# A four-layer gated cross-attention kernel: where the second layer's blocks stand in their slots, and how the last output tiles wait

## What is computed

```
queries = rope(q @ Wq.T)            # 32 heads of 128
keys    = rope(ctx @ Wk.T)          # 8 key heads, each serves 4 query heads
values  = ctx @ Wv.T
scores  = queries @ keys.T * 128 ** -0.5, causal mask (256 x 256)
x = x + tanh(g) * (softmax(scores) @ values) @ Wd.T
```

## Time and profile before

| what | us |
|---|---|
| median of 3 runs (lowest, highest) | 2197.25 (2195.84, 2198.91) |
| the profiled execution, its own time | 2194.48 |
| its span in the profile | 2192.7 |
| TensorE matmul busy | 1983.3 |
| VectorE busy | 1470.3 |
| ScalarE busy | 1026.8 |
| GpSimd busy | 927.6 |

### The profile page before, as it was taken

One profiled execution on the slowest core, in us unless ns is written; L12 is line 12 of the kernel. 1 busy time (PEld: TensorE's weight loads), 2 busy tenths in 40 slices (PEclk: granted clock), 3 DMA queues, 4 the chain that ended last, 5 costly groups with the idle time before them and its releaser, 6 DMA issues.

```text
span 2192.7 us, 33276 instructions
## 1 busy us (share of the span) xinstructions
PE 1983.3 (90%) x10874; PEld 1660.7 (76%) x10874; DVE 1470.3 (67%) x2725; ACT 1026.8 (47%) x2264; POOL 927.6 (42%) x971
## 2 busy tenths in 40 slices
PE   5999999999747999997997999997889999999998
PEld 4788888887536777776665888886678888888886
DVE  5777777777767777776423555555557766777676
ACT  3666666666414444444112544443145545555542
POOL 2555455544535555455231323322234444444432
PEclk9999999999968999999997999999799999999999
DMA  3212222121310211111110101001101110111001
GB/s 137 64 54 73 87 72 72 47 84 54 97 34 30 78 48 52 48 48 54 48 55 25 33 9 32 17 10 55 53 10 44 44 45 15 44 45 44 16 25 45
DMA packets 47069, 106.77 MB, mean 49 GB/s; under 512 B 6064, under 2 KB 21936, under 8 KB 43104
## 3 DMA queue, kind: packets, MB, share of 16 engines
q1 hardware_dynamic: 46944, 105.14, 15.1%
HBM read 98.37 MB, written 6.75 MB: 48 GB/s over the span
## 4 chain that ended last, share of the span: by engine, by line
PE 64%; DVE 18%; ACT 9%; issue 7%; POOL 1%; ACTq 0%; DVEq 0%; POOLq 0%
PE psX L369 22%; PE psQ L369 13%; PE psS L369 11%; PE psO L369 10%; PE psT L752 5%; DVE pT_lo L906 2%; ACT pT_hi L1083 1%; DVE dq_space L461 1%; PE psT L369 1%; DVE nmax L894 1%; ACT dq_space L448 1%; DVE p_sb L888 1%; DVE nbias L892 1%; ACT oT_hi L1105 1%; ACT p_sb L1076 1%
## 5 line engine op out<-in xcount | busy, mean ns | idle before, releaser
L1191 POOL TENSOR_SCALAR p_sb<-p_sb,rrec 128x512 f32<-128x512 f32 (+1 forms) x320 | 265.9, 831 | 701.7 <-DVE rrec L902 701.6
L1083 ACT ACTIVATE pT_hi<-psT 128x512 fp32r<-128x512 f32 (+2 forms) x384 | 235.0, 612 | 381.4 <-PE psT L752 381.3
L906 DVE TENSOR_TENSOR pT_lo<-psT,pT_hi 128x512 fp32r<-128x512 f32 (+2 forms) x384 | 271.4, 707 | 81.4 <-ACT pT_hi L1083 81.4
L369 PE MATMUL psO<-pT_hi,v_hi 128*128 128x256 f32 (+1 forms) x832 | 255.6, 307 | 70.6 <-DVE oT_lo L927 33.8
L752 PE MATMUL psT<-ident,p_sb 128*128 128x128 f32 x1600 | 242.4, 276 | 13.7 <-POOL p_sb L1191 10.5
L369 PE MATMUL psO<-pT_lo,v_hi 128*128 128x256 f32 (+1 forms) x832 | 237.4, 285 | 0.0
L369 PE MATMUL psO<-pT_hi,v_lo 128*128 128x256 f32 (+1 forms) x832 | 237.3, 285 | 0.0
L752 PEld LDWEIGHTS psT<-ident,p_sb 128*128 128x128 f32 x1600 | 195.0, 142 | 53.1 <-POOL p_sb L1191 15.9
L369 PEld LDWEIGHTS psO<-pT_hi,v_hi 128*128 128x128 f32 (+1 forms) x832 | 155.2, 187 | 85.9 <-issue 40.3
L1076 ACT ACTIVATE p_sb<-psS,nbias 128x512 f32<-128x512 f32 (+1 forms) x192 | 145.3, 757 | 126.5 <-DVE nbias L896 126.5
L369 PE MATMUL psS<-kT_hi,q_hi 128*128 128x512 f32 (+2 forms) x448 | 177.3, 396 | 27.1 <-ACT p_sb L1076 18.7
(11 more groups left out here) (337 smaller groups left out, 4785.3 us busy)
## 6 DMA issues: line engine op xcount, KB each, us to landing
wq_f<-in_a_wq SPq DMA_DIRECT2D x96, 256.0 KB, 2.7
wo_f<-in_a_wo SPq DMA_DIRECT2D x24, 1024.0 KB, 6.8
wkv_f<-in_a_wkv SPq DMA_DIRECT2D x24, 512.0 KB, 4.0
mask_sb<-in_codes SPq DMA_DIRECT2D x32, 174.0 KB, 2.4
qscr<-in_amax SPq DMA_DIRECT2D x32, 174.0 KB, 2.3
w<-qscr SPq DMA_DIRECT2D x32, 174.0 KB, 1.9
wo_f<-in_f_wT SPq DMA_DIRECT2D x3, 1024.0 KB, 4.9
wq_f<-in_a_wq SPq DMA_DIRECT2D x16, 192.0 KB, 2.3
```

What stands on the lines that cost most here:

```text
L369: mm = pe.matmul(dst, w, m, start=(first and k == 0), stop=(last and k == n - 1))
L906: L.t_lo.inc(dve.tensor_tensor(pT_view(L, pT_lo, j), t_view(L, j), pT_view(L, pT_hi, j).bitcast(F32), ALU.subtract))
L1083: L.t_hi.inc(act.activation(pT_view(L, pT_hi, j), t_view(L, j), ACT.Copy))
L1191: L.s_norm.inc(pool.tensor_scalar(p_view(L, j), p_view(L, j), rrec[:, j:j + 1], 1.0, ALU.mult, ALU.mult))
```

## The change

Second layer: `q_slot` from (1, 1, 1, 1) to (0, 0, 1, 0), so that the query blocks of heads 0, 1 and 3 stand in the first slot; v0 from (2,1) to (3,0) and t0 from (3,0) to (3,1). ScalarE's o_high goes ahead of row_exp, VectorE's o_low ahead of row_recip, and kT_lo, left over from an earlier slot, ahead of the query work; q_front waits for VectorE's own q_low, since both use qscr. The three copies in VectorE's tail of the second layer go behind o_low. In all layers the first of the last output tiles waits for oT_lo head by head.

```diff
@@ -63,9 +63,9 @@
-    dict(kind="rope", hd=128, groups=8, keys=256, slots=2, nbuf=2, ahead=2, settle=2, q_slot=(1, 1, 1, 1),
+    dict(kind="rope", hd=128, groups=8, keys=256, slots=2, nbuf=2, ahead=2, settle=2, q_slot=(0, 0, 1, 0),
          outs=OUT_PAIRS, splits=SPLIT_PAIRS,
-         prep={(2, 0): ["k0"], (2, 1): ["v0"], (3, 0): ["t0"]}),
+         prep={(2, 0): ["k0"], (3, 0): ["v0"], (3, 1): ["t0"]}),
@@ -778,10 +778,13 @@
                 if kind in ("out", "end"):
-                    L.o_lo.wait(pe, gp.at(4, 4))
                     L.wo_lo.wait(pe, gp.at(4, 4))
-                    mm = three(pe, X, [([oT_view(L, z, gp, h)[:, i * P:(i + 1) * P] for z in (0, 1)],
-                                        [z[0:hd, h, :] for z in (wo_hi, wo_lo)]) for h in range(G4)])
+                    for h in range(G4):
+                        if h == 0 or what == ("end", 0):
+                            L.o_lo.wait(pe, gp.at(4, h + 1 if kind == "end" else 4))
+                        mm = three(pe, X, [([oT_view(L, z, gp, h)[:, i * P:(i + 1) * P] for z in (0, 1)],
+                                            [z[0:hd, h, :] for z in (wo_hi, wo_lo)])],
+                                   first=(h == 0), last=(h == G4 - 1))
@@ -908,6 +911,7 @@
             def q_front(g, h):
                 L.q_mm.wait(dve, g.at(4, h + 1))
+                L.q_lo.wait(dve, g.at(4, h) if g.off or g.loop is not None or h else 0)
                 L.q_f.inc(rotated(dve, psQ[:, :], qscr))
@@ -1016,17 +1020,22 @@
                     pT_low(g, h, j)
-                    if L.step(g, h, j, L.settle):
-                        row_recip(*L.step(g, h, j, L.settle))
+                    settled = L.step(g, h, j, L.settle)
+                    if settled and not L.pairs:
+                        row_recip(*settled)
                     if j == 0 and (h or g.off or g.loop is not None):
                         o_low(*((g, h - 1) if h else (g.to(-1), 3)))
+                    if settled and L.pairs:
+                        row_recip(*settled)
+                    before = list(late)
+                    while L.rope and late:
+                        k_low(*late.pop(0))
                     if j == 0 and L.rope and L.head(g, h, 2):
                         q_low(*L.head(g, h, 2))
...
-                    before = list(late)
@@ -1039,13 +1048,13 @@
-                elif L.i == 1:
+                elif L.i == 2:
+                    f2_router(dve)
+                o_low(g, 3)
+                if L.i == 1:
                     f1_up_high(dve, 0)
                     f1_up_high(dve, 1)
                     f1_down_high(dve, 0)
-                elif L.i == 2:
-                    f2_router(dve)
-                o_low(g, 3)
@@ -1150,10 +1159,12 @@
-                    if nxt:
+                    if nxt and not L.pairs:
                         row_exp(*nxt)
                     if j == 0 and (h or g.off or g.loop is not None):
                         o_high(*((g, h - 1) if h else (g.to(-1), 3)))
+                    if nxt and L.pairs:
+                        row_exp(*nxt)
```

## The result

The changed kernel takes **2159.8 us** (median of 4 runs, 2158.6 to 2160.4) against 2197.4 for the kernel before: a ratio of 0.983, 95% interval 0.981 to 0.985, 37.5 us less. Forecast were 2151 us, 46.5 less. The profiled execution took 2159.55 us, its span is 2157.8.

A forecast was written before the change was run, and what follows sets the result against it. TensorE, busy nine tenths of the span, was taken as the bound, with waits in the second layer; 23.7 + 4.2 + 4.0 + 6.0 + 1.0 + 4.3 + 3.3 = 46.5 us less gave 2151 us, range 2138 to 2172.

The forecast's parts named there:

- the signs that the prediction set for itself: Right: 44 us group, only a 1.5 to 2 us kT_lo wait; wrong: 46 us or more, or 0.63 us matmuls.
- Outputs ahead of exponentials, blocks in first slots: Second layer's steady groups: the 3.23 and 1.30 us waits for oT_lo go.
- The next wait: Slot (3,0), second layer: TensorE waits 1.75 us for kT_lo, in place of 0.98.
- VectorE takes TensorE's place: Rival, second layer: VectorE runs further behind, pT_lo late every second slot, 2 us more a group, 2165 us; chance 0.22.
- catching up in head 1: Second layer's groups: VectorE, behind through heads 2, 3 and 0, catches up in head 1, which has four blocks (14.5 us).
- Six groups: Second layer's steady groups: 44.0 us each in place of 47.95, 23.7 us saved over six, before the clock's 6.0.
- The clock: Second layer's steady groups: TensorE no longer falls to 1.2 GHz, returning all 6.0 us.
- The first group and the one after: Second layer: query blocks cover the first group's waits, 4.0 us; the stretch before the six follows their pattern, 4.2.
- The ends: Second layer's last group 1.0 us and last output tiles 4.3; last tiles of first and third layers 1.65 and 1.6.
- either case of the forecast: Second layer's three copies in the tail: gain 4.3 us, or 5.3 if the first copy shortens to 0.43 by the port rule.
- psX would start at once: Second layer's last output tiles: nine matmuls of the first three heads start without the 3.52 us wait.
- the 7.6: Last output tiles of all layers: 1.7 us in the first, 4.3 second, 1.6 third, none in the fourth.

The follow-up runs named there:

- kT_lo late: The changed kernel with kT_lo behind the query rotation again, as before the change; ratio 0.9886 to the kernel before.
- values back: The changed kernel with the values block back at (2,1), behind the query block, transposes staying at (3,1); 2162.7 us, ratio 0.9850 to the kernel before.
- only the queries moved: The changed kernel with values back at (2,1) and transposes at (3,0), so only the queries' slots are new; 2165.7 us, ratio 0.9859.
- split of wq first: The changed kernel with GpSimd splitting wq ahead of the keys' sum in the second layer; 2152.4 us, ratio 0.9801 to the kernel before.
- tails alone: The kernel before with only the layer ends changed (head-by-head wait, second layer's copies behind the last o_low); ratio 0.9971.
- old slots, new order: The changed kernel with query, values and transposes slots of before; new order within slots and tails stay; ratio 0.9921 to the kernel before.
- exponentials first: The changed kernel with exponentials ahead of o_high and the reciprocal ahead of o_low again; ratio 0.9902 to the kernel before.
- one reduction more, in head 3: The changed kernel plus an unused 0.69 us VectorE reduction in slot (3,0) of each group but the last; 2163.7 us, ratio 0.984.
- one reduction more, in head 1: The changed kernel plus an unused 0.69 us VectorE reduction in slot (1,1) of each group but the last; 2157.6 us, ratio 0.981.
- values back, split of wq first: The changed kernel with the values block back at (2,1) and GpSimd's wq split ahead of the keys' sum; 2153.5 us, ratio 0.9804.
- VectorE's work to head 1, both forms: The changed kernel with wq split first, keys at (1,0), values at (2,1), queries in first slots (second form: head 1's in its second); 2152.7 and 2153.8 us.

## Why the prediction was right, and where it was off

The direction, the mechanism in the second layer and the range held; the gain was forecast at 46.5 us and is 35 between the two profiles, 37.5 between the medians. That the range held owes something to its width: of the signs that the prediction set for itself, the place of the wait and the end of those for oT_lo came, but the wait is 2.16 us (1.5 to 2 forecast), the group 44.9 (44), and one steady group of six has the lower clock and 0.63 us matmuls, which was named as a sign of being wrong. Point by point, with the times of the two profiles:

**Outputs ahead of exponentials, blocks in first slots.** Right: no wait for oT_lo is left in a steady group. Parts of the change undone show both to be needed: slots alone leave 0.44 to 0.72 us and a later VectorE, order alone leaves 2.60.

**The next wait.** The keys' wait was named, with its place, at 1.75 us in all; it is 2.16 + 0.25. The chain (rotation, sum, kT_hi, kT_lo) ran in the forecast order. Mis-sized was one step: kT_lo at 0.69 us took 1.37, since in its new place it meets GpSimd's split of wo. With the split out of its way it took 0.76 and the group lost 0.64 us. Of the 0.87 us by which the group is too long, 0.41 are the wait, 0.15 its restart (the sum put it at 0.1, where it takes 0.25 elsewhere in the same text) and 0.3 gaps too short to show as waits in the rows. A rule on the port that the two engines share, which I had weighed for the copies only, bears here. The Trainium skill, Advanced Engine Details and Errata, section GPSIMD Details, says that GpSimd shares a read and a write interface with VectorE and conflicts there with VectorE instructions that have two SBUF inputs. kT_lo has two, and the rows agree: the one that starts second is the one that grows, kT_lo by 0.68 us here, GpSimd's sum by 0.5 us in the kernel with kT_lo late.

**VectorE takes TensorE's place**, the rival given 0.22, names what bounds the group better than the forecast did. I treated the keys' chain and VectorE's load as two limits. They are one: with the keys' wait covered, the same 44.9 us came back as a wait for pT_lo (values back, only the queries moved), and 0.6 us less of VectorE showed wherever TensorE waited. Its size was overstated (2 us a group; the group is 44.9, not 44.0 and not 46), because the hand-followed schedule already held most of it. Half right too was the catching up in head 1: an addition there is hidden.

**Six groups.** Forecast 29.7 us with the clock, measured 290.86 - 267.80 = 23.1. Of the missing 6.6, six by 0.87 are the group's length (44.87 for 44.0) and 1.4 the clock.

**The clock.** All 6.0 us were taken back in the forecast, because it never fell after waits of 1.3 and the longest was to be 1.75; the wait became 2.16, and it fell once in six groups. With the wait at 1.54 us (split of wq first) it fell in none of five, so the length of the wait matters. It does not decide alone: with the same 2.15 us it fell in four of five groups of another kernel (values back). That it cost only 1.4 us here, and not most of the 6.0, is nothing that the forecast had a reason for.

**The first group and the one after.** Forecast 4.0 and 4.2, measured 28.34 - 23.52 = 4.8 and 43.87 - 43.36 = 0.5. The second term failed. It copied the steady pattern, but the first group has no output tiles, so VectorE has no head 1 in which to catch up. It came into slot (2,0) late, TensorE waited 2.13 us for pT_lo there, and the next block ran at the lower clock, at 0.63 us a matmul (0.96 in that row). Together the forecast was 2.9 us too high.

**The ends.** Last group and tail: forecast 1.0 + 4.3 = 5.3, measured 32.64 - 28.09 = 4.55. Up to the last product it is 0.1 in place of 1.0, as TensorE went to the lower clock at 1001.2, behind five waits of 0.2 to 0.8 us; the first matmuls of psX still ran at it (0.76 and 0.51 us). From there on it is 4.5: the copies took 2.2 us, less than either case of the forecast, the first two 0.75 together with GpSimd idle for most of it, the third 1.52 beside its split of wq. That psX would start at once left out its wait for wo_lo, which cost 1.06 us with the tails alone. First layer: 1.65 forecast, some 1.75 measured; the tails alone brought 6.4 of the 7.6. In the third layer the 1.6 came, but its last heads lost 3.2 us before it: from the scores at 1452.02 (1489.69 before) to the last product's last matmul TensorE took 30.56 us, 27.39 before, and its rows are at the lower clock from the start (granted clock 0.70 in the first row below, of the changed kernel; 0.95 in the second, from the same place of the kernel before, with 59 matmuls in the time of 44). The change touches nothing in these heads, and nothing of it was in the sum. All these points make 33 of the 35 us between the two profiles; the rest lies in stretches that the change does not touch.

```profile
1452.00:1463.00 11.00, 9.20 (x44) 8.49 (x45) 4.48 (x10) 4.29 (x8) 3.08 (x4) 0.70 0.00 0
```

```profile
1489.67:1500.67 11.00, 9.20 (x59) 8.05 (x60) 5.58 (x12) 5.14 (x10) 5.21 (x5) 0.95 0.01 1
```

## What to carry to other kernels

When a wait of the engine that bounds is covered, ask whether the engine it waited for is late at this one place or late throughout: put a block in front of the wait, and see whether the stretch gets shorter or the wait turns up further on. Where two engines are both busy for over eight tenths of a stretch, spread each one's blocks so that the second has its light stretch soon after its heavy one; filling the first engine's empty slots alone stops at the second's pace. (Spreading was tried here in two forms and brought 0.3 us a group, so it is the less proven half of the advice.) And an instruction moved in time meets other work on the ports it shares: look at what the neighbour engine does in the new place, and which of the two starts first, not only at the row's duration in the old one.

## What was not expected of the hardware

A subtraction of two SBUF tiles on VectorE (kT_lo, 512 columns) took 1.37 us where a two-input instruction of GpSimd was under way and ran until 0.5 us before its end. It took 0.76 us where that instruction was over (split of wq first), and 0.69 us where it started 0.05 us before one, which then took 1.78 us in place of 1.3 (kT_lo late). The wait after which TensorE's clock fell was shorter than the kernel before suggested. By the longest wait of a steady group, with the number of the first five steady groups that had the lower clock:

| kernel | longest wait, us | groups at the lower clock |
|---|---|---|
| tails alone | 3.25 | 4 of 5 |
| before | 3.25 | 3 of 5 |
| kT_lo late | 3.25 | 3 of 5 |
| only queries moved | 2.7 | 3 of 5 |
| old slots, new order | 2.7 | 5 of 5 |
| exponentials first | 2.5 | 4 of 5 |
| one reduction more, in head 3 | 2.17 | 2 of 5 |
| one reduction more, in head 1 | 2.17 | 2 of 5 |
| values back | 2.16 | 4 of 5 |
| the change | 2.16 | 1 of 5 |
| split of wq first | 1.55 | 0 of 5 |
| values back, split of wq first | 1.50 | 0 of 5 |
| VectorE's work to head 1, both forms | 1.24 | 0 of 5 |

The length alone does not decide, since the clock fell in more groups with the values back than with kT_lo late; but in no kernel here did it fall in a steady group whose longest wait was under 1.6 us. Outside the steady groups it did fall with shorter single waits, as at the end of the second layer of the changed kernel (0.93 from 987.37 to 1003.35, no wait there over 0.82 us, five of them within 5 us). In the groups where it fell, waits of 2 to 3 us cost 0.7 to 1.6 us more than themselves, so a small edit that shortens one can return more than its length.
